# Second experts: adding a tile into the output by halves of its rows instead of halves of its columns

## What is computed

```
x = x + 0.5 * ffn(layernorm(x))      # first experts
x = x + attention(layernorm(x))
x = x + 0.5 * ffn(layernorm(x))      # second experts

ffn: logits = x @ router_w.T                       # 8 experts
     topk_vals, topk_idx = top_k(logits, 2)
     weights = softmax(topk_vals)
     expert_out[e] = (silu(x @ w1[e]) * (x @ w2[e])) @ w3[e]     # 512 -> 256 -> 512
     out[token] = sum over its two experts of weight * expert_out[expert][token]
```

## Time and profile before

| what | us |
|---|---|
| median of three runs | 1292.87 (1291.17 to 1295.96) |
| the profiled execution | 1295.78 |
| its span in the trace | 1294.5 |
| granted TensorE clock over the span | 0.986 of full speed |
| first add of the second experts starts | 1089.63 |
| last add starts | 1290.88 |
| POOL busy in its 78 adds | 127.1 |

### The profile page before, as it was taken

How to read it: one execution, slowest core, us unless ns; L and a number is a source line. 1 busy time by engine, 2 the same in 40 slices (tenths; PEclk the granted TensorE clock), 3 DMA queues, 4 the chain that set the end, 5 groups by cost and what they waited for, 6 DMA issues and landing times.

```text
span 1294.5 us, 22123 instructions
## 1 busy us (share of the span) xinstructions
PE 1202.9 (93%) x7422; PEld 781.6 (60%) x7429; DVE 897.0 (69%) x2100; ACT 661.0 (51%) x1313; POOL 602.1 (47%) x496
## 2 busy tenths in 40 slices
PE   4899999989998999999999999989999989999996
PEld 3578888758776554444545455545444447777774
DVE  7767777679996666575667677587754685666664
ACT  2545555525546554354456566356567733444442
POOL 5835445314200111001426556465682373888886
PEclk9899999999999999999989999999999999999999
DMA  9923333565620032023345845656743353666665
GB/s 345 354 90 109 105 114 107 163 181 104 109 48 32 4 68 34 1 96 50 86 124 139 164 99 111 183 131 157 138 99 66 109 210 74 104 103 101 101 103 73
DMA packets 68557, 148.52 MB, mean 115 GB/s; under 512 B 8832, under 2 KB 29312, under 8 KB 64448
## 3 DMA queue, kind: packets, MB, share of 16 engines
q0 software_dynamic: 35184, 93.34, 34.2%
q1 hardware_dynamic: 33264, 53.77, 12.1%
HBM read 81.28 MB, written 33.55 MB: 89 GB/s over the span
## 4 chain that ended last, share of the span: by engine, by line
PE 60%; DVE 17%; DMA 9%; issue 7%; POOL 4%; ACT 3%; SPq 0%; DVEq 0%; POOLq 0%; ACTq 0%
PE bank L1637 10%; PE bank L839 9%; PE bank L1649 9%; PE bank L997 8%; PE bank L862 5%; PE bank L1667 4%; PE bank L1704 3%; DMA out<-Y,DI 3%; DMA XG<-xn,TK 3%; POOL out L789 3%; DVE PM L1010 3%; DVE bank L1012 2%; PE bank L821 2%; PE bank L1398 2%; DMA CD<-P 1%
## 5 line engine op out<-in xcount | busy, mean ns | idle before, releaser
L1756 ACT ACTIVATE P<-bank 128x512 f32<-128x512 f32 (+3 forms) x640 | 303.8, 535 | 259.4 <-PE bank L1637 252.7
L1010 DVE TENSOR_REDUCE PM<-bank 128x1 f32<-128x512 f32 x384 | 252.8, 686 | 82.5 <-PE bank L997 81.9
L1637 PE MATMUL bank<-Qs,Ks 98*128 98x512 f32 (+3 forms) x640 | 241.1, 407 | 5.0 <-ACT P L1756 2.8
L997 PE MATMUL bank<-Ks,Qs 96*128 96x512 f32 (+3 forms) x640 | 234.6, 387 | 10.7 <-DVE PM L1012 5.4
L1637 PEld LDWEIGHTS bank<-Qs,Ks 98*128 98x128 f32 x640 | 116.9, 190 | 130.8 <-issue 59.5
L1795 POOL TENSOR_SCALAR_AFFINE_SELECT P<-P 128x512 f32<-128x512 f32 x64 | 42.9, 682 | 284.6 <-ACT P L1756 234.9
L1012 DVE CUSTOM_DVE_ANT_0 bank<-bank,KB 128x128 f32<-128x128 f32 (+3 forms) x256 | 124.8, 499 | 56.5 <-PE bank L997 55.9
L997 PEld LDWEIGHTS bank<-Ks,Qs 96*128 96x128 f32 x640 | 121.5, 191 | 57.6 <-DVE PM L1010 17.3
L1649 PE MATMUL bank<-P,V 128*32 128x512 f32 (+3 forms) x1280 | 150.9, 543 | 3.9 <-POOL P L1795 3.9
L789 POOL DMA_INDIRECT out<-Y,DI x78 | 127.1, 1629 | 40.7 <-issue 33.9
L1809 POOL TENSOR_TENSOR CH<-CH,P 128x512 f32<-128x512 f32 x108 | 139.3, 1438 | 14.0 <-ACT P L1756 13.3
(11 more groups left out here) (190 smaller groups left out, 1987.8 us busy)
## 6 DMA issues: line engine op xcount, KB each, us to landing
CD<-P POOLq DMA_DIRECT2D x17, 1024.0 KB, 7.3
xn<-XN SPq DMA_DIRECT2D x8, 1024.0 KB, 7.1
WR<-L_ffn_w POOLq DMA_DIRECT2D x16, 512.0 KB, 15.4
XO<-y POOLq DMA_DIRECT2D x8, 1024.0 KB, 9.8
WR<-L_ffn_w SPq DMA_DIRECT2D x16, 512.0 KB, 8.4
CD<-P SPq DMA_DIRECT2D x7, 1024.0 KB, 5.2
CD<-CH POOLq DMA_DIRECT2D x7, 1024.0 KB, 7.0
XA<-y POOLq DMA_DIRECT2D x24, 256.0 KB, 4.2
```

Of the source, the lines that this page charges most:

```text
L997: pe.matmul(bk(g, bank)[:, 0:n], g.Qs[b][0:96, G % 4 * 4 + h, c * P:c * P + P], g.Ks[0:96, G % 4, k * BQ:k * BQ + n], start=True, stop=Tru ...
L1010: dve.tensor_reduce(dst, bk(g, bank)[:, 0:n], AX.X, ALU.max).then_inc(s(f"free{bank}"), 1)
L1637: pe.matmul(bk(g, bank)[:, o:BQ], g.Ks[0:98, G % 4, k * P:k * P + P], g.Qs[G // 4][0:98, G % 4 * 4 + j, o:BQ], start=True, stop=True).then ...
L1756: act.activation(a.P4[buffer_of(n)][:, j, o:BQ], bk(g, score_bank(g, i))[:, o:BQ], ACT.Exp, scale=scale).then_inc(s("exp"), 1)
```

## The change

Three things. The adds of a tile are now its rows 0 to 63 (h = 0) and its rows 64 to 127 (h = 1), each with all 512 columns: 64 rows of 2 KB. Two tiles may share tokens in any of their rows, so both adds of tile j stand behind the landing of both adds of tile j-1: `added(g, pool.wait_ge, j - 1)` waits for both semaphores ahead of add(j, 0), and add(j, 1) has no wait of its own but Y's, which has already passed. gather(j+4) now stands behind add(j, 1) instead of between the two adds. The row numbers of rows 64 to 127 are brought down to partitions 0 to 63 by one small DMA on SP (semaphore `lower`), and dve_route makes one list of row numbers in one instruction instead of TF and two lists in three.

```diff
@@ route_memory
-    if f == 0:
-        r.DI = small("DI0", [P, NJ], U32)
-    else:
-        r.TF = small("TF1", [P, NJ])
-        r.DI2 = small("DI1", [P, 2, NJ], U32)
+    r.DI = small(f"DI{f}", [P, NJ], U32)
+    if f:
+        r.DH = small("DH1", [P // 2, NJ], U32)
@@ dve_route
-    if f == 0:
-        dve.tensor_tensor(r.DI[:], r.TD[:], sl[:, 0:NJ], ALU.add).then_inc(rt.sem, 1)
-    else:
-        dve.tensor_tensor(r.TF[:], r.TD[:], sl[:, 0:NJ], ALU.add).then_inc(rt.sem, 1)
-        dve.wait_ge(rt.sem, rt.up())
-        for h in range(2):
-            ins = dve.tensor_scalar(r.DI2[:, h, :], r.TF[:], 2.0, float(h), ALU.mult, ALU.add)
-        ins.then_inc(rt.sem, 1)
+    dve.tensor_tensor(r.DI[:], r.TD[:], sl[:, 0:NJ], ALU.add).then_inc(rt.sem, 1)
@@ pool_experts
     def add(j, h):
+        rows = slice(64 * h, 64 * h + 64)
         pool.wait_ge(s("y"), b + j + 1)
-        if j == 0 and h == 0:
-            before_adding()
-        elif j:
-            pool.wait_ge(s(f"add_{h}"), 16 * j)
+        if j == 0:
+            before_adding(h)
+        elif h == 0:
+            added(g, pool.wait_ge, j - 1)
         pool.indirect_dma_start(
-            out=g.out.rearrange("t (h d) -> (t h) d", h=2),
-            out_offset=bass.IndirectOffsetOnAxis(ap=r.DI2[:, h, j:j + 1], axis=0),
-            in_=x.Y[:, j % 3, h * FF:h * FF + FF], in_offset=None, compute_op=ALU.add).then_inc(s(f"add_{h}"), 16)
+            out=g.out[:, :], out_offset=bass.IndirectOffsetOnAxis(ap=(r.DH if h else r.DI)[0:64, j:j + 1], axis=0),
+            in_=x.Y[rows, j % 3, :], in_offset=None, compute_op=ALU.add).then_inc(s(f"add_{h}"), 16)
@@
         else:
             add(j, 0)
+            add(j, 1)
             if j + NG < NJ:
                 gather(j + NG)
-            add(j, 1)
@@ sp_down1
     load_down(g, 1, sp)
+    sp.wait_ge(s("route1"), g.routed[1]["DI"])
+    sp.dma_start(g.r[1].DH[:], g.r[1].DI[P // 2:P, :]).then_inc(s("lower"), 16)
@@ build
-        def residual_stored():
-            pool.wait_ge(s("stored"), 64)
-            pool.wait_ge(s("dump"), 16)
+        def residual_stored(h):
+            if h:
+                pool.wait_ge(s("lower"), 16)
+            else:
+                pool.wait_ge(s("stored"), 64)
+                pool.wait_ge(s("dump"), 16)
```

## The result

The changed kernel takes 1338.05 us, median of four runs (1334.93 to 1339.5); the kernel before on the same chip took 1294.29. The ratio is 1.0327 with a 95% interval of 1.0306 to 1.0348: 3.3% slower, where 1285.7 was forecast. The profiled execution has a span of 1338.2, against 1294.5.

The account below looks back on a forecast made before the run. POOL, full with DMA issues, was taken to bound the second experts. First add at 1089.63, first round 6.93, 37 rounds of 5.05 (186.85) and 3.96 end at 1287.4, 7.1 less; from the median, 1285.7. Range 1277 to 1302.

Parts of the forecast that it names:

- (1) Issue, A = 0.96: POOL's issue of one half-tile add, second experts: falls from 1.58 to 0.96 us with 64 rows; bounds 0.79 to 1.58.
- (1) Transfer, 0.88 for 1.20: Transfer of a 64-row half's add: 0.88 us instead of 1.20, so 0.32 gained in each landing.
- a slow first round: Second experts, first add of tile 0 to that of tile 1: 6.93 us, against 6.64 before.
- disturbed adds and the gather: Additions to each chain round: 0.10 us for disturbed adds, raising 4.90 to 5.00, then the gather's limit, giving 5.05.
- (2) The new chain: add(j, 0) waits for add(j-1, 1): a tile takes at least A + 0.30 + A + 2.68 = 4.90 us.
- (3) The gather: Gather behind the second add delays PE: 9.5 to 10.2 us over two tiles, 4.8 to 5.1 a tile; round taken as 5.05.
- if it does in most, the moved gather is the limit: Sign to check: PE waiting for the gather in most tiles would show the moved gather as the limit.
- (4) Small things: Routing's single list of row numbers and one DMA on SP: about 0.3 us less routing that nobody feels; counted 0.
- PE took over: Rival: with A = 0.79 the chain, 4.56, falls under PE's 4.874 a tile; 16.0 us less, 1276.9; chance 0.18.
- The half by rows does not travel worse: Denies the rival that 64 partitions transfer slower: 1320 if 8 engines serve a half, 1298.2 without gain; chance 0.12.
- the rival on the other side: Issue barely falls, two issues lie in every round: slower from A = 1.05, 1302.7 at 1.2, 1325 at 1.49; chance 0.16.
- POOL's busy time in 50 us: Sign to check in the second experts: POOL's busy time in 50 us falls from 41 to about 30.

Follow-up runs that it names:

- e1_forms: Changed kernel with other forms of the add by tile (16 to 128 rows, 1 or 2 KB, accumulating or plain); 1332.08 in a single run, compared with nothing.
- e2_joint: Kernel before, column halves kept, but both adds wait for both landings of the tile before and the gather is last; 1342.44, ratio 1.0394.
- e5_full: Changed kernel with one add of 128 rows x 2 KB per tile behind the landing of the tile before, gather behind it; 1313.57, ratio 1.0142.
- e8_between: Changed kernel with the gather back between its two adds; 1384.08, ratio 1.0696 to the kernel before.
- e3_own: Changed kernel, second half added into table y, each half waiting only for its own landing, gather between adds; output lacks half the rows; 1283.73, ratio 0.9935.
- e4_own_last: Changed kernel with only the waits and second half's target changed: own landings, table y, gather still last; 1291.15, ratio 0.9991.
- e6_moved: Kernel before with only the gather moved behind both adds, each column half keeping its own chain; 1301.42, ratio 1.0052.

## Why the prediction was wrong

The mechanism that the prediction put at the bottom of its sum was right: a round is the first add's issue, 0.30, the second add's issue and the way from there to the next first add. Two terms of it were mis-sized, and both errors were on the same side.

- **(1) Issue, A = 0.96: this step failed.** It is 1.416 on the mean of 78. A counts 78 times, 35.5 us of the 50.8 by which the end of the span was missed (1338.2 against 1287.4). The prediction took the middle of two guesses, one of which fitted the indirect add through the fixed 0.67 of the direct accumulating DMAs. e1_forms shows a fixed 1.26. That 0.96 is near a plain write of 128 rows was no support for it: that is another kind of DMA. The row to go by was there: a plain write of as many rows, indexed in the same way, took 1.00 against 1.58. The prediction laid this extra of 0.58 on the rows for its value, and had it as a fixed price only in its bound, 1.49, which was within 0.07 of the truth.
- **(1) Transfer, 0.88 for 1.20: failed.** The two row halves took 18.0 engine-us each (time summed over the 16 DMA engines), against 19.2 for a column half: in 19.7 us at the end of the stage the queue was busy for 34.3% of 16 engines, 108.1 engine-us for 6 adds. So 1.13, not 0.88. The price of a row came from DMAs that accumulate into SBUF, 28.1 for 128 x 2 KB. Into HBM the same work took more, and by bytes: six column halves of e2_joint took 17.4 each (33.9% of 19.3 us x 16), and three whole tiles of e5_full, 128 x 2 KB, 33.4 each (38.4% of 16.3 us x 16). The rows for it, of the kernel after, e2_joint and e5_full; the first is the busy share of the 16 engines in the 19.7 us by fortieths, in tenths:

```profile
DMA  0000095809910000000069419640000009728750
q0 software_dynamic: 480, 0.79, 34.3%
...
q0 software_dynamic: 864, 0.79, 33.9%
...
q0 software_dynamic: 432, 0.79, 38.4%
```

  From the second add's issue to the next first add there were 3.06 in the median and 3.19 on the mean, not 2.68. In 38 rounds that is 19.4 us: 12.2 are the 0.32 of shorter transfer that did not come, most of the rest is the long landings and the one late start behind a usual landing. The sum held 7.6 against it under other names: 2.0 for a slow first round, which took 6.66 and not 6.93, and 5.6 for disturbed adds and the gather (0.15 a tile), which were not needed. So 11.8 of the miss are left here. A later start, 2.7, and 0.6 in the tail make up the rest of the 50.8, but for 0.2.
- **(2) The new chain: right.** With the measured A the formula as written, but with 3.0, gives 2 x 1.42 + 0.30 + 3.00 = 6.14; the median round is 6.19. e2_joint (6.46 worked out, median 6.45), e8_between (the gather's 1.32 added) and e3_own (the chain gone, and the loss with it) show it from three sides.
- **(3) The gather: right as a limit, of no effect here.** The sum over two tiles held to about 2% in e4_own_last (5.17 for 5.28); e6_moved gave 5.56 in its profile and some 5.43 in the median, about the 5.3 to 5.45 that was expected. In the kernel after, the chain of 6.3 lies above it. One sign was wrong: "if it does in most, the moved gather is the limit". PE waited for the gather in nearly every tile and the gather was not the limit. A wait of an engine behind the chain tells nothing of what holds the chain; the releaser of the first add does.
- **(4) Small things: nothing, as said.** DH's DMA was issued at 1076.37, wanted at 1094.15, and waited for by nobody.
- **The rivals.** PE took over only in e3_own, where A was 1.4 and the chain was cut. The half by rows does not travel worse: its 18.0 engine-us lie between the 17.4 and 19.2 of column halves, the DMA row above has slices in which the 16 engines are busy to 90% or more, where 8 engines would stop at half, and the way from the second add's issue to the next first add is 3.06, where fewer engines were to show 3.5. What came true was the rival on the other side, that the issue barely falls, with its place and its turning point (A = 1.05). It stood at 0.16 and at 1325 for A = 1.49. It was too low even there because it too used the shorter transfer; with 3.0 it would have been 12 more, 1337. That this is within 1 of the result would have been in part luck: 1.49 for 1.416 is 5.8 us too many, and makes up for long landings and the later start. POOL's busy time in 50 us, 30.65 where about 30 was forecast, is luck as well: longer issues in fewer rounds.

The upper end of the range went wrong with the same step: 1302 was A = 1.2 with the short transfer, though 1.49 and 1.58 and the full 1.20 stood in the text as bounds. When a term counts 78 times and its bounds are 0.7 apart, the range has to hold most of that, some 50 us.

Open: whether the "instruction" packets make the long landings that they go with; why POOL starts 1.2 late in one round near the end, in the kernel after and likewise in e2_joint; and how much of e5_full's 5 us above its range is the longer issues, how much the waits for Y.

## What to carry to other kernels

Count the waits for a landing that stand one behind another, and what is issued between them. Two transfers that each wait for their own predecessor hide a chain of 4.6 (issue, landing, restart) in a round of 5.1; the same two behind a common wait pay both issues and the landing, 6.3 to 6.5. Halving the rows of a DMA whose issue is mostly fixed (here 1.26 of 1.58) buys a tenth, so a form that the trace doesn't show is to be costed from the nearest DMA of the same kind, and its extra over a plain one taken as fixed until shown otherwise.

## What was not expected of the hardware

- The issue of an indirect accumulating DMA on POOL did not depend on its bytes: 1.57 for 256 KB and 1.58 for 128 KB, both of 128 rows. 16 rows, an eighth, still took 1.30.
- An indirect accumulation into HBM took 18.0 engine-us for 64 rows of 2 KB and 17.4 to 19.2 for 128 rows of 1 KB, nearly the same for the same bytes, and 33.4 for 128 rows of 2 KB; direct ones into SBUF took 14.1 for 64 rows of 2 KB.
- An indirect DMA that POOL began to issue during DVE's DL, an instruction with two inputs in SBUF, often took longer: eleven adds of e5_full 1.65 to 2.07 for 1.59.
